# Attention maxima carried by a free bias row instead of a pick product

## What is computed

```python
attn = jnp.einsum('bnhd,bmhd->bhnm', q * scale, k)
attn = attn + bias.transpose(2, 0, 1)[None]      # bias: (64, 64, heads), from a table
attn = jax.nn.softmax(attn, axis=-1)
out = jnp.einsum('bhnm,bmhd->bnhd', attn, v)
```

## Time and profile before

| | us |
|---|---|
| median of 3 runs (323.93 to 325.02) | 324.87 |
| the profiled execution | 324.21 |
| its span, first to last instruction | 322.4 |
| PE busy | 289.2 |
| DVE busy | 235.0 |
| ACT busy | 203.0 |
| POOL busy | 107.3 |

### The profile page before, as it was taken

One profiled execution on the slowest core, in us unless ns is written; L12 is line 12 of the kernel. 1 busy time (PEld: TensorE's weight loads), 2 busy tenths in 40 slices (PEclk: granted clock), 3 DMA queues, 4 the chain that ended last, 5 costly groups with the idle time before them and its releaser, 6 DMA issues.

```text
span 322.4 us, 6206 instructions
## 1 busy us (share of the span) xinstructions
PE 289.2 (90%) x2314; PEld 211.3 (66%) x2314; DVE 235.0 (73%) x456; ACT 203.0 (63%) x343; POOL 107.3 (33%) x144
## 2 busy tenths in 40 slices
PE   2648979999999999999989797898999999999993
PEld 2236766878878686886868543453577777777772
DVE  4867437589798888979787336679999999976211
ACT  6696633948667685865535788987953746754400
POOL 4151425756576567555441601231310000000000
PEclk9986989999999999999979999999999999999998
DMA  6870383434244333424430000590008659767811
GB/s 162 178 156 31 84 188 85 104 76 90 71 98 89 78 84 76 103 67 96 101 71 2 0 2 0 115 212 14 2 0 169 130 113 196 141 137 147 182 33 33
DMA packets 17276, 29.94 MB, mean 93 GB/s; under 512 B 5536, under 2 KB 12192, under 8 KB 17248
## 3 DMA queue, kind: packets, MB, share of 16 engines
q1 hardware_dynamic: 13792, 22.72, 30.9%
q0 software_dynamic: 2880, 6.03, 11.0%
q10 hardware_dynamic: 576, 0.81, 1.0%
HBM read 4.22 MB, written 2.10 MB: 20 GB/s over the span
## 4 chain that ended last, share of the span: by engine, by line
PE 76%; DVE 7%; ACT 5%; SPq 4%; DMA 4%; issue 2%; POOL 0%; DVEq 0%; ACTq 0%
PE psum L1089 27%; PE psum L868 13%; PE psum L791 5%; PE psum L865 5%; PE psum L884 5%; PE psum L1013 3%; PE psum L844 3%; DVE maxima L1209 3%; SPq L379 3%; PE psum L1001 3%; PE psum L813 3%; DMA k_heads<-k_parts 3%; PE psum L892 2%; PE psum L818 2%; PE psum L823 2%
## 5 line engine op out<-in xcount | busy, mean ns | idle before, releaser
L1089 PE MATMUL psum<-shifted,conv_w 128*128 128x512 f32 x336 | 86.5, 419 | 0.0
L1089 PEld LDWEIGHTS psum<-shifted,conv_w 128*128 128x128 f32 x336 | 63.9, 191 | 21.6 <-issue 1.3
L868 PEld LDWEIGHTS psum<-q_heads,k_blocks 128*128 128x128 f32 x384 | 56.1, 194 | 6.5 <-issue 3.0
L868 PE MATMUL psum<-q_heads,k_blocks 128*128 128x256 f32 x384 | 57.3, 286 | 0.0
L1209 DVE TENSOR_REDUCE maxima<-psum 128x8 f32<-128x512 f32 x64 | 40.1, 683 | 12.2 <-PE psum L844 12.0
L603 ACT ACTIVATE probs<-psum 128x512 f32<-128x512 f32 x64 | 37.5, 603 | 18.2 <-PE psum L868 18.0
L461 POOL DMA_DIRECT2D k_blocks<-k_parts x56 | 32.2, 583 | 11.5 <-PE psum L868 11.5
L865 PE MATMUL psum<-minus_max,pick 128*128 128x512 f32 x64 | 32.7, 511 | 0.5 <-ACT probs L603 0.3
L844 PE MATMUL psum<-k_heads,q_blocks 128*128 128x256 f32 x128 | 24.0, 314 | 9.5 <-DMA k_heads<-k_parts 6.9
L791 PE MATMUL psum<-parts,center_average 128*128 128x512 f32 x64 | 22.6, 436 | 8.7 <-DVE parts L287 7.1
L287 POOL TENSOR_TENSOR parts<-x,parts 128x256 fp32r<-128x256 f32 (+1 forms) x21 | 19.4, 938 | 32.0 <-ACT parts L552 22.2
(11 more groups left out here) (142 smaller groups left out, 468.1 us busy)
## 6 DMA issues: line engine op xcount, KB each, us to landing
shifted<-images SPq DMA_DIRECT2D x32, 332.5 KB, 5.5
q_heads<-q_parts SPq DMA_DIRECT2D x128, 32.0 KB, 2.2
k_blocks<-k_parts POOLq DMA_DIRECT2D x56, 64.0 KB
k_heads<-k_parts SPq DMA_DIRECT2D x64, 32.0 KB, 2.3
out<-x SPq DMA_DIRECT2D x8, 256.0 KB, 4.8
q_blocks<-q_parts POOLq DMA_DIRECT2D x28, 64.0 KB, 2.5
x<-in_x SPq DMA_DIRECT2D x6, 256.0 KB, 6.2
x<-in_x SPq DMA_DIRECT2D x4, 128.0 KB, 4.0
```

The lines of the kernel that those rows point to most:

```text
L868: ins = pe.matmul(bank[:, hh * G // 2:(hh + 1) * G // 2], k_blocks[:, hh, w // (NW // 2), k_part, w % (NW // 2), :], of_half(q_heads[:, q_ ...
L1089: ins = pe.matmul(psum[:, CONV0 + bh, :], conv_w[bh][:, w_part, t, :], img[:, y:y + H - 1:2, x0:x0 + W], start=t == 0 and w_part + part == ...
```

## The change

One bias row of each half is made free: all bias rows are taken relative to one key position, whose own row is then zero on the queries' side. This row (partition 64 for the first half of heads, partition 0 for the second) now holds the maxima: those of batch half 0 in the place of the rounded part, those of batch half 1 in the place of the rest; the keys' side of the row holds 0, -1 or +1, so that the six products that stay also subtract the right maximum. The pick product, `pick`, `minus_max` and `maxima_t` go. The maxima are transposed in two parts of 32 rows (four windows each) behind the keys, copied by DVE to `gauge` in two operations, and placed by four DMAs of 16 runs of 512 B per group: two issued by ACT behind the key evacuation, two by POOL behind the key blocks. The first part uses the bank of the weighted values, so these now wait for its copy. `q_heads` and `q_parts` change their order in memory. At the start a third load (128 partitions of 8 runs of 256 B) brings the row that is subtracted, and POOL sets the free rows with four small memsets.

```diff
+def _key_rows():
+    r = ((_p % T)[:, None] == T - 1 - _p % T).astype(np.float32)
+    r[_p % T == 0] = -(_p >= T).astype(np.float32)
+    return r
...
-    "head_of_row": (_p % NH)[:, None] == np.arange(NH),
-    "window_of_row": C * ((_p // NH % NW)[:, None] == np.arange(NW)),
+    "key_rows": _key_rows(),
-        maxima_t = sb("maxima_t", [128, T])
+        gauge = sb("gauge", [128, 2, 2 * T], F32R)
-        q_heads = at("q_heads", [128, 2, NH, G], F32R)
+        q_heads = at("q_heads", [128, 2, NH, NW // 2, 2, T], F32R)
-        q_parts = at("q_parts", [128, 2, 2, G], F32R)
+        q_parts = at("q_parts", [128, 2, NW, 2, T], F32R)
+        def maxima_bank(s):
+            return psum[0:32, MAX0, 0:128] if s else psum[0:32, PV, 256:384]
+        FREE_ROWS = ((0, T), (1, 0))
+        def send_gauge(engine, n, s):
+            engine.wait_ge(S["dv_gauge"], 2 * n + s + 1)
+            if isinstance(n, int) and n == 0:
+                engine.wait_ge(S[f"q_heads_set{s}"], 1 + s)
+            else:
+                engine.wait_ge(S["pe_scores"], NW * (n - 1) + (s + 1) * NW // 2)
+            for hh, row in FREE_ROWS:
+                engine.dma_start(q_heads[row:row + 1, s, heads_of(hh)].rearrange("o h w l t -> o (h w) (l t)").bitcast(F32),
+                                 gauge[hh * 16:(hh + 1) * 16, s, :].bitcast(F32)).then_inc(S[f"gauge_in{s}"], 16)
...
             load_bias(1, "rel_table")
+            sp.dma_start(rel_base.rearrange("p (a f) -> p a f", a=WS), bass.AP(d["rel_table"].tensor, d["rel_table"].offset, [[0, 128], [side * NH, WS], [1, WS * NH]])
+                         ).then_inc(S["rel_in1"], 16)
...
-            pool.tensor_tensor(pick[:], const("average").unsqueeze(1).to_broadcast([128, NW, 128]),
-                               const("window_of_row").unsqueeze(2).to_broadcast([128, NW, 128]), ALU.mult).then_inc(S["po_pick"], 1)
+            for hh, row in FREE_ROWS:
+                for bh, sign in ((0, -1.0), (1, 1.0)):
...
+                    pool.memset(k_blocks[row:row + 1, hh, :, 1, :, bh * T:(bh + 1) * T].bitcast(F32), sign).then_inc(S["key_rows_set"], 1)
...
                     key_blocks(nxt, 1 - par, 1)
+                    send_gauge(pool, nxt, 1)
...
                     evacuate_k(far, par)
+                if nxt is not None:
+                    send_gauge(act, nxt, 0)
                 if prev is not None:
                     inverse_deviation2(prev)
...
-            def transpose_maxima(n):
-                pe.wait_ge(S["dv_max"], NW * (n + 1))
-                pe.matmul(psum[0:C, MAX0, 0:128], maxima[:], const("ident"), start=True, stop=True).then_inc(S["pe_maxt"], 1)
+            def transpose_maxima(n, s):
+                pe.wait_ge(S["dv_max"], NW * n + (s + 1) * NW // 2)
+                if s == 0 and not (isinstance(n, int) and n == 0):
+                    pe.wait_ge(S["dv_turned"], 2 * n - 1)
+                pe.matmul(maxima_bank(s), maxima[:, s * 32:(s + 1) * 32], const("ident"), start=True, stop=True).then_inc(S["pe_maxt"], 1)
...
-                if w == 0:
-                    pe.wait_ge(S["dv_minus"], g + 1)
...
                     pe.wait_ge(S[f"q_heads_in{w // (NW // 2)}"], 16 * NH * (g + 1))
+                    pe.wait_ge(S[f"gauge_in{w // (NW // 2)}"], 32 * (g + 1))
                 bank = psum[:, PROB0 + w % 2, :]
-                pe.matmul(bank, pick[:, w, :], minus_max[:, :, :], start=True, stop=False)
...
+            def weighted_values(g, quad, par, nxt=None):
+                if quad == 1 and nxt is not None:
+                    pe.wait_ge(S["dv_gauge"], 2 * nxt + 1)
...
-            def spread_maxima(n):
...
+            def round_maxima(n, s):
+                dve.wait_ge(S["pe_maxt"], 2 * n + s + 1)
+                if not (isinstance(n, int) and n == 0):
+                    dve.wait_ge(S[f"gauge_in{s}"], 32 * n)
+                dve.tensor_copy(gauge[0:32, s, :], maxima_bank(s)).then_inc(S["dv_gauge"], 1)
...
-            def low_of_bias():
...
+            def queries_bias():
+                dve.wait_ge(S["rel_in1"], 48)
+                dve.tensor_tensor(square_rows(rel_whole), patches(1), rel_base.rearrange("p (a b h) -> p h a b", a=WS, b=WS),
+                                  ALU.subtract).then_inc(S["dv_rel_whole"], 1)
+                dve.wait_ge(S["dv_rel_whole"], 1)
+                dve.tensor_copy(rel_high, rel_whole).then_inc(S["dv_rel_high"], 1)
+                dve.wait_ge(S["dv_rel_high"], 1)
+                low_part(dve, rel_whole, rel_high, rel_low).then_inc(S["dv_rel_low"], 1)
```

More of the change, by code:

```diff
@@ L185, in conv_seq_kernel @@
         rel_raw = scratch[:, NRAW:NRAW + 2 * NH * PATCH].rearrange("p (n f h) -> p n f h", n=2, h=NH)
+        rel_base, rel_whole = (scratch[:, NRAW + 2 * NH * PATCH + i * NH * T:NRAW + 2 * NH * PATCH + (i + 1) * NH * T] for i in range(2))
         qkv_raw, proj_raw, mlp1_raw = (raw[:, a:b] for a, b in _RAT.values())
@@ L303, in low_of_square, with by_window, heads_of @@
             low_part(engine, square, parts[:, 0, :], parts[:, 1, :]).then_inc(S["square_low"], 1)
+        def by_window(t):
+            return t.rearrange("p (w t) -> p w t", t=T)
+        def heads_of(half):
+            return slice(half * (NH // 2), (half + 1) * (NH // 2))
         def halves(t):
@@ L330, in query_rows @@
         def query_rows(part, half, windows):
-            rows = of_half(q_heads[:, part], half).rearrange("p h (w t) -> p h w t", t=T)
-            return rows[:, :, windows.start:windows.stop, :]
+            return q_heads[:, windows.start // (NW // 2), heads_of(half), :, part, :]
         QUADRANTS = [(hh, bh, slice(hh * 64 + bh * 32, hh * 64 + bh * 32 + 32)) for hh in range(2) for bh in range(2)]
@@ L388, in spread_queries @@
                 sp.wait_ge(S["dv_q_low"], n + 1)
-                some = slice(half * G // 2, (half + 1) * G // 2)
+                some = slice(half * NW // 2, (half + 1) * NW // 2)
                 for h in range(NH):
-                    sp.dma_start(of_head(q_heads, h)[:, :, h, some].bitcast(F32), of_head(q_parts, h)[:, n % 2, :, some].bitcast(F32)
+                    sp.dma_start(of_head(q_heads, h)[:, half, h].rearrange("p w l t -> p (w l t)").bitcast(F32), of_head(q_parts, h)[:, n % 2, some].rearrange("p w l t -> p (w l t)").bitcast(F32)
                                  ).then_inc(S[f"q_heads_in{half}"], 16)
@@ L582, in evacuate_q @@
                     act.wait_ge(S["q_blocks_in"], 64 * (n - 2))
-                act.activation(q_parts[:, par, 0, :], psum[:, MISC0, :], ACT.Identity, bias=q_bias[:, 0:1]).then_inc(S["ac_q_high"], 1)
+                act.activation(q_parts[:, par, :, 0, :], by_window(psum[:, MISC0, :]), ACT.Identity, bias=q_bias[:, 0:1]).then_inc(S["ac_q_high"], 1)
             def first_query_blocks():
@@ L663, in _ @@
             for half in range(2):
-                ins = act.activation(k_blocks[:, half, :, 0], reversal().rearrange("p (s w) t -> p s w t", s=2), ACT.Copy, scale=not_in_half(half))
+                ins = act.activation(k_blocks[:, half, :, 0], reversal("key_rows").rearrange("p (s w) t -> p s w t", s=2), ACT.Copy, scale=not_in_half(half))
             ins.then_inc(S["k_blocks_set"], 1)
@@ L859, in scores @@
                     pe.wait_ge(S["k_blocks_in0"], 64 * (g + 1))
+                    if isinstance(g, int) and g == 0:
+                        pe.wait_ge(S["key_rows_set"], 4)
                 if w == NW // 2 and not (isinstance(g, int) and g == 0):
```

74 lines of the change are left out of this document (37 added, 37 removed).

## The result

The changed kernel takes 334.04 us (median of 4 runs, 331.28 to 335.12), the kernel before beside it 324.40 us (4 runs, 323.54 to 325.02): a ratio of 1.030, 95% interval 1.026 to 1.034. It is slower. The forecast of 321.2 us was wrong, and its range, 317.5 to 327.0, does not hold the time. The rival "the row lands late", given 0.12 and 328.9 us, is what happened, with a higher price. The profiled execution took 333.0 us, span 331.2.

A forecast was written before the change was run, and what follows sets the result against it. A loop of waits over DVE and ACT, not PE's work, was taken as the bound. Step gains 1.8 + 0.6 + 1.1 + 0.5 + 0.4 = 4.4, less 0.7, gave 3.7 us: median 321.2, range 317.5 to 327.0.

The forecast's parts named there:

- the row lands late: Rival, each step's first scores: each microsecond of landing beyond 2.9 costs one in 7 steps; 328.9 us at 4.0; chance 0.12.
- What bounds the kernel: Attention steps: a loop DVE, ACT, DVE closes in 18.53 of 18.98 us whatever PE saves, so 0.45 us gained per step.
- The wait for the landed rows: Before each step's first scores: rows land in a median 2.3 us; stall 0.0 to 1.0 us, 0 taken.
- It is a quarter of the size of those copies: Argument against late landing: the row is smaller than the 32 KB copies within SBUF that took up to 3.4 us.
- the copy of 4.68 us under load: Key landing near 40 us, at 4.68 us after issue; cited as support for a late row.
- ACT's cover: Before ACT rounds x1: its waits of 0.35 us for PE and 0.25 for DVE cover landings up to about 2.9 us.
- ACT's issues: Two DMAs before the second norm's logarithm, 0.41 us each, eat DVE's 0.55 us relief; net +0.14 to -0.36, 0.0 taken.
- given back on ACT: Rival: ACT's issues cost 0.59 us each, as SP's, and the start loses 1.5: 324.2 us, no change; chance 0.14.
- POOL at no cost: POOL's two issues behind the key blocks, 1.16 us, fit its 2.21 us wait before rounding x: cost nothing.
- The start: Kernel start: the third bias load delays the key copies that the first maxima need, 0 to 1.5 us, 0.7 taken.
- The sum: Whole kernel: gains of 4.4 us over the attention steps, less 0.7 at the start, give 3.7 us.
- The small terms: Gains outside steps 2 to 6: 0.4 us in step 0, 0.6 in step 1, 0.5 in step 7.

The follow-up runs named there:

- Two orders with the same work: Against the kernel with the first half early (320.38 us, step 18.64), second norm's variance product, logarithm and exponential ahead of keys, division ahead of second copy: 317.19 us, step 17.99.
- the emptied queues: Against the changed kernel, POOL's rows go ahead of its key blocks and SP's second-half query copies wait until ACT's rows land: 354.01 us.
- the kernel with the first half early: Against the changed kernel, the first four maxima are transposed and copied before the last are taken, ACT issuing their rows ahead of the key evacuation: 320.38 us.
- the kernel with 16 partitions: Against the changed kernel, scores do not wait for the rows, which go into 16 partitions of an unread place instead of one row: 325.55 us.

## Why the prediction was wrong

**What bounds the kernel: right in the main.** A loop of waits was the bound, and not PE's work. Two orders with the same work differ by 0.65 us a step. When nothing new was waited for, four middle steps went from 75.89 to 74.22 us (0.41 us a step) while PE's busy time in them fell by 1.12 us a step; first before, then with all rows issued by POOL and not awaited (stretch, length, PE):

```profile
71.36:147.25 75.89, 73.88 (x897) 58.59 (x898) 65.57 (x125) 54.22 (x105) 48.12 (x69) 1.00 0.39 85
...
70.87:145.09 74.22, 69.39 (x874) 53.77 (x872) 61.71 (x121) 54.41 (x105) 58.75 (x85) 1.00 0.40 88
```

The loop is not DVE and ACT alone: in the second kernel DVE still waits 0.22 us before the fifth maximum, and 1.27 us for PE's weighted values, where it waited 0.77 before; PE itself waits 0.43 us there for POOL.

**The wait for the landed rows: the step that failed.** I took a landing of 2.3 us, the median of SP's query copies, and a stall of 0. Landings of 3.0 to 4.4 us followed in seven of eight steps, most of them above the 3.4 us that those larger copies took at most. The timing of the step was otherwise as worked out: from the transposes' start to the second issue 113.28 - 112.06 = 1.22 us (1.01 forecast), to PE ready for the scores 115.81 - 112.06 = 3.75 us (3.36). So the row had 2.53 us to land, and took 4.02. "It is a quarter of the size of those copies" was the argument against the rival, and size was the wrong measure: step 0's 2.16 us and the 1.91 us of the emptied queues are about this row's own time, 3.0 to 3.1 us is what it took beside POOL's key blocks and SP's copies, and 3.6 to 4.4 us where an instruction packet was in flight too. For that I had the better row in hand, the copy of 4.68 us under load, and used it for the rival alone. The Trainium skill (DMA: Bandwidth & Descriptors, Anatomy of one DMA — SWDGE (gpsimd) path) puts a DMA from GpSimd at 2.0 us plus bytes over 436,000 per us, an estimate of 2.02 us for 8 KB; POOL's rows ahead of its key blocks agree in the median (1.9 us, with 4.0 at most).

**ACT's cover was no cover.** I counted ACT's two waits, 0.35 and 0.25 us, against a late row. They stand behind the exponentials that the late scores delay. The delay reached DVE whole: in the step shown DVE waits 3.40 us at the residual addition, behind 1.63 us of waiting for the row and about 1.5 us of slow clock. What the wait cost, 10.6 us, is about PE's 11.5 us of waiting; the rival's price, 1 us for each beyond 2.9, gives (3.75 - 2.9) x 7 = 6.0 us. Of the difference the slow clock after one such wait is 1.5 us; the rest isn't split.

**ACT's issues: the term mis-sized.** 0.41 us each was taken from issues at the start, with 0.59 as the upper end. Two took 1.15 us, 0.58 each: SP's price, of the copies that are like them, and not that of the loads from HBM. Then "given back on ACT" follows as it was worked out: 324.2 us, no change, against 323.44 us measured without the row's wait (323.94 for the kernel before beside it). I also missed that PE's queries wait for the logarithm (0.38 us in the step shown). In step 5 this was the larger loss: the second issue alone took 1.93 us, and the queries waited 1.71 us for the logarithm, the scores only 0.41 us for the row.

**POOL at no cost: right** at its place. Its rounding of x, ready to start at 114.26, still waits 1.73 us for ACT after the two issues. The cover has an end: eight issues between the maxima and the rounding, in place of two, cost 1.20 us of PE's time.

**The start: mis-sized, and of no weight.** The first max product came 1.8 us later in the profile (26.59 against 24.79), not 0.7. Taking the load away moved it back by 1.4 us, in the kernel with the first half early, and left the total.

**The sum.** Without the two waits the change gives 320.06 or 320.38 us, against 323.5 for the kernel before in the same runs: a gain of 3.1 to 3.4 us where the sum said 3.7. In the profile of the first, steps 2 to 5 give 1.7 us (forecast 1.8) and step 6 gives 1.9 (1.1). The small terms were luck: step 0 is 3.0 us shorter and step 1 2.7 us longer (DVE's first copies at 32.10, 53.14 and 71.36 us before, 31.96, 49.97 and 70.87 there), where 0.4 and 0.6 were to be gained. The middle steps were right, and one wait that was taken as nothing was 10.6 us.

## What to carry to other kernels

When a value that went from engine to engine is sent through a DMA, price the trip by the slowest copy that the trace shows under the same traffic, not by the median of its kind, and give it that time by issuing it from the first moment at which its data exist. Put the issues where their engine waits for something else: two issues behind a dependency cost 0.6 us a step, inside an old wait nothing. A wait of another engine covers a delay only if it isn't itself behind the delayed work.

## What the runs showed of the hardware

- An 8 KB copy within SBUF landed after 1.7 to 1.9 us with little beside it, and after up to 4.4 us with 64 KB and 32 KB copies in flight; writing 16 partitions in place of one row didn't change that (4.1 us at most).
- With SP and POOL held back, loads of instructions show up as DMA packets in the same stretches as slow landings (about 1 us of one engine in step 2), in the four slow ones of seven and in none of the three quick ones. In the changed kernel, with all the other copies in flight, the landings with such a packet of q8 took 3.58 to 4.38 us and those without 2.16 to 3.10 us.
- SP's 24 issues of a step, which I had put at 14.2 us, took 16.9 to 18.2 us when it never waited (in the kernel with 16 partitions, 45.72 to 62.62 and 62.71 to 80.91 us), so SP is close behind the loop; in step 1 there PE waited 2.05 us for the keys.
